# Transposes ahead of the product in the last stage of a six-layer kernel

## The reference

```python
def bitlinear158(x, w, b):
    xq = act_quant(rms_norm(x))      # round(x * 127 / max|x|), 8-bit levels
    wq = weight_quant(w)             # -1, 0, 1 times a scale
    return jnp.einsum('bsd,od->bso', xq, wq) + b
...
h = jax.nn.silu(bitlinear158(x, w1, b1))          # 256 -> 1024
h = jax.nn.gelu(h, approximate=False)
h = layer_norm(h, ln_g, ln_b)
return bitlinear158(h, w2, b2)                    # 1024 -> 256
```

## Time and profile before

| | |
|---|---|
| Time, median of 3 runs | 704.51 us |
| The three runs | 700.71, 704.51, 704.6 us |
| Profiled execution: span from first to last instruction | 711.1 us |
| Profiled execution: a time of its own beside the span | none is given |
| Mean granted TensorE clock of the profiled execution | 0.944 |
| Share of the span: TensorE, VectorE, ScalarE, GpSimd | 87%, 73%, 56%, 47% |
| Second half of the feed-forward, first gelu to the end | 617.4 to 711.1 us |

### The profile page before, as it was taken

One profiled execution on the slowest core, in us unless ns is written; L12 is line 12 of the kernel. 1 busy time (PEld: TensorE's weight loads), 2 busy tenths in 40 slices (PEclk: granted clock), 3 DMA queues, 4 the chain that ended last, 5 costly groups with the idle time before them and its releaser, 6 DMA issues.

```text
span 711.1 us, 15833 instructions
## 1 busy us (share of the span) xinstructions
PE 617.1 (87%) x4620; PEld 471.5 (66%) x4622; DVE 518.5 (73%) x1187; ACT 399.1 (56%) x826; POOL 335.0 (47%) x650
## 2 busy tenths in 40 slices
PE   6999999989998899689999689999999677557776
PEld 5788888875555764477887567888887433245554
DVE  3688999985999674125224569999999578688994
ACT  2577777773333133034332246777777467778992
POOL 1234655444997344411112445333332568475882
PEclk9899999999999799799999779999999899859999
DMA  8301400011348701432221310000000000000101
GB/s 290 129 3 36 168 0 0 0 32 29 67 67 347 260 0 53 141 127 75 78 86 43 142 38 24 2 3 0 0 0 1 1 1 1 0 0 1 35 25 60
DMA packets 23043, 42.07 MB, mean 59 GB/s; under 512 B 3056, under 2 KB 18048, under 8 KB 21840
## 3 DMA queue, kind: packets, MB, share of 16 engines
q1 hardware_dynamic: 19504, 31.14, 13.9%
q0 software_dynamic: 3488, 10.28, 4.3%
HBM read 31.15 MB, written 10.26 MB: 58 GB/s over the span
## 4 chain that ended last, share of the span: by engine, by line
PE 55%; issue 14%; DVE 14%; POOL 8%; ACT 7%; DVEq 1%; DMA 1%; another core or an unknown queue 0%; SPq 0%; POOLq 0%; ACTq 0%
PE ps L1229 6%; PE ps L335 5%; PE ps L363 5%; PE ps L373 4%; PE ps L1109 4%; PE ps L383 3%; PE ps L322 3%; POOL ctx_sb L891 3%; PE ps L345 3%; DVE work L577 3%; PE ps L1239 3%; PE ps L802 2%; PE ps L1162 2%; DVE work L583 2%; PE ps L1883 2%
## 5 line engine op out<-in xcount | busy, mean ns | idle before, releaser
L498 ACT COPY wide<-ps 128x512 f32<-128x512 f32 x126 | 74.5, 593 | 43.3 <-PE ps L335 41.3
L230 POOL TENSOR_TENSOR var_eps<-mv,powers 128x1 f32<-128x1 f32 x80 | 16.8, 210 | 160.6 <-DVE mv L221 160.5
L577 DVE TENSOR_REDUCE work<-ps 128x8 f32<-128x1024 f32 x64 | 77.9, 1217 | 15.4 <-PE ps L322 12.1
L335 PE MATMUL ps<-ident,work 128*128 128x128 f32 x512 | 76.2, 281 | 3.9 <-ACT wide L498 1.8
L493 ACT ACTIVATE work<-work 128x1024 f32<-128x1024 f32 x64 | 68.4, 1069 | 20.0 <-DVE work L583 19.5
L583 DVE TENSOR_TENSOR work<-ps,work 128x1024 f32<-128x1024 f32 x64 | 77.8, 1216 | 0.6
L335 PEld LDWEIGHTS ps<-ident,work 128*128 128x128 f32 x512 | 59.2, 144 | 20.5 <-issue 14.3
L363 PE MATMUL ps<-xnT,w_qkv 128*128 128x128 f32 x256 | 41.0, 309 | 10.8 <-DVE work L583 9.3
L1275 POOL DMA_DIRECT2D sorted_y<-work x23 | 13.6, 591 | 78.0 <-DVE work L1270 78.0
L233 POOL TENSOR_TENSOR rstd<-var_eps,powers 128x1 f32<-128x1 f32 x80 | 45.1, 564 | 6.3
L1883 PE MATMUL ps<-w_o,wide 128*128 128x128 f32 x256 | 34.7, 294 | 15.0 <-DVE w_o L1929 15.0
(11 more groups left out here) (226 smaller groups left out, 1572.9 us busy)
## 6 DMA issues: line engine op xcount, KB each, us to landing
wide<-in_expert_gu SPq DMA_DIRECT2D x1, 4096.0 KB, 15.3
sorted_x<-small POOLq DMA_DIRECT2D x1, 2944.0 KB, 11.7
work<-sorted_x SPq DMA_DIRECT2D x23, 128.0 KB, 2.0
sorted_y<-work POOLq DMA_DIRECT2D x23, 128.0 KB, 2.0
xn_all<-in_ctx_rev_t SPq DMA_DIRECT2D x1, 2048.0 KB, 10.6
small<-hank SPq DMA_DIRECT2D x16, 128.0 KB, 3.8
w_qkv<-hank SPq DMA_DIRECT2D x16, 128.0 KB, 3.8
wide<-in_expert_d SPq DMA_DIRECT2D x1, 2048.0 KB, 9.9
```

The costliest lines, as they stand in the source:

```text
L335: mm = pe.transpose(turned(t, r)[:, h * P:(h + 1) * P], prob[r][:, h * P:(h + 1) * P], ident)
L498: act.copy(probT[r], turned(t, r)).then_inc(s["pT"], 1)
L577: dve.tensor_reduce(mxs[:, 8 * g:8 * g + 8], S2[g], AX.X, ALU.max).then_inc(s["mx"], 1)
```

## The change

In `pe_second` the two blocks of a step change places: `T(t-1)` stands before `Y(t-2)`. ScalarE's `int`, in both halves of the feed-forward, becomes a copy with a constant bias where it was an identity with a bias read from a column. In the first tiles: GpSimd runs `mean(1)` before `rstd(0)`; ScalarE's `var(1)` waits for the mean of tile 1 alone; tile 0's moments have a semaphore of their own, and VectorE goes on to `centred(0)` without counting up `mean` and `var`; the thresholds of the waits on these two follow. In VectorE's step 1 `diag(0)` stands before `ln(1)`. An unused semaphore goes.

```diff
@@ act_first
-                    act.activation(qT[u][:, 0:D], TB[u][:, 0:D], ACT.Identity, bias=c_nmagic
+                    act.activation(qT[u][:, 0:D], TB[u][:, 0:D], ACT.Copy, bias=-MAGIC
...
@@ act_int
-                act.activation(qT[u], TB2[u], ACT.Identity, bias=c_nmagic).then_inc(s["qT"], 1)
+                act.activation(qT[u], TB2[u], ACT.Copy, bias=-MAGIC).then_inc(s["qT"], 1)
@@ act_second
                 if there(t + 1):
-                    act.wait_ge(s["mean"], 2 * (t + 2))
+                    act.wait_ge(s["mean"], 2 * (t + 1))
...
@@ pe_second
-                if there(t - 2):
-                    pe.wait_ge(s["qT"], NB + t - 1)
-                    wait(pe, s["x_new"], t - 3)
-                    for c in range(8):
-                        mm = pe.matmul(Y[u][:, 0:D], qT[u][:, c * P:(c + 1) * P], wq[1][:, c, :],
-                                       start=(c == 0), stop=(c == 7))
-                    mm.then_inc(s["y_ps"], 1)
                 if there(t - 1):
...
                     mm.then_inc(s["qT_ps"], 1)
+                if there(t - 2):
+                    pe.wait_ge(s["qT"], NB + t - 1)
+                    wait(pe, s["x_new"], t - 3)
+                    for c in range(8):
+                        mm = pe.matmul(Y[u][:, 0:D], qT[u][:, c * P:(c + 1) * P], wq[1][:, c, :],
+                                       start=(c == 0), stop=(c == 7))
+                    mm.then_inc(s["y_ps"], 1)
@@ dve_moments
-                dve.bn_aggr(f.mv_buf[:, 0:2], f.bn_buf).then_inc(s["mean"], 2)
-                dve.wait_ge(s["mean"], 2)
-                dve.engine_nop().then_inc(s["var"], 1)
+                dve.bn_aggr(f.mv_buf[:, 0:2], f.bn_buf).then_inc(s["moments"], 1)
+                dve.wait_ge(s["moments"], 1)
@@ dve_second (dve_ln and dve_diag are the old lines, made functions)
+                early = isinstance(t, int) and t == 1
+                if early:
+                    dve_diag(dve, 0, 0)
                 if there(t):
+                    dve_ln(dve, t, u)
+                if there(t - 1) and not early:
+                    dve_diag(dve, t - 1, 1 - u)
@@ gpsimd
-                pool_rstd(pool, 0, 0, f.var[0])
                 pool_mean(pool, 1, 1)
+                pool_rstd(pool, 0, 0, f.var[0])
```

More of the change, by code:

```diff
@@ L175, in build @@
         moe_loaded = sem("moe_loaded")
-        zero_stored = sem("zero_stored")
         out_stored = sem("out_stored")
@@ L1574, in feed_forward @@
                 "factor", "rounded", "diag", "qT_ps", "qT", "h_ps", "silu", "gelu", "mean",
-                "var", "eps2", "rstd", "centred", "ln", "y_ps", "x_bias", "x_new", "h_bias", "unscale")}
+                "var", "eps2", "rstd", "centred", "ln", "y_ps", "x_bias", "x_new", "h_bias", "unscale",
+                "moments")}
             w32 = [xn_all[:, 0:2048], xn_all[:, 2048:4096]]
@@ L1834, in act_gelu @@
             def act_gelu(act, t, u):
-                wait(act, s["mean"], 2 * (t - 1))
+                wait(act, s["mean"], 2 * (t - 2))
                 act.activation(Ht(t), Ht(t), ACT.Gelu, accum_out=hsum[u]).then_inc(s["gelu"], 1)
@@ L1851, in act_second @@
                 if there(t + 2):
-                    wait(act, s["mean"], 2 * (t + 1))
+                    wait(act, s["mean"], 2 * t)
                 if there(t + 1):
@@ L1863, in act_second @@
                     wait(act, s["eps"], NB + t)
-                    wait(act, s["var"], min(t + 2, NB))
+                    wait(act, s["var"], min(t + 1, NB - 1))
                     act.activation(junk, Ht(t), ACT.Square, scale=INNER ** -0.5, accum_out=ms[u]
@@ L1898, in dve_moments, with dve_ln, dve_diag @@
                 dve.wait_ge(f.bn_done, f.base + NB + 2)
-                dve.bn_aggr(f.mv_buf[:, 0:2], f.bn_buf).then_inc(s["mean"], 2)
-                dve.wait_ge(s["mean"], 2)
-                dve.engine_nop().then_inc(s["var"], 1)
+                dve.bn_aggr(f.mv_buf[:, 0:2], f.bn_buf).then_inc(s["moments"], 1)
+                dve.wait_ge(s["moments"], 1)
+            def dve_ln(dve, t, u):
+                dve.wait_ge(s["rstd"], t + 1)
+                dve.wait_ge(s["centred"], t + 1)
+                dve.scalar_tensor_tensor(Ht(t), Ht(t), rstd2[u], ln_b, ALU.mult, ALU.add
+                                         ).then_inc(s["ln"], 1)
+            def dve_diag(dve, t, u):
+                dve_largest(dve, t, u, 1)
+                dve_inverse(dve, t, u, 1)
+                dve.wait_ge(s["inverse"], NB + t + 1)
+                dve.wait_ge(s["rms127"], NB + t + 1)
+                wait(dve, s["qT_ps"], NB + t - 1)
+                dve.tensor_scalar(diag[u], ident, inverse[u], rms127[u], ALU.mult, ALU.mult
+                                  ).then_inc(s["diag"], 1)
             def dve_second(dve, t, u, i):
                 if there(t):
-                    dve.wait_ge(s["var"], t + 1)
+                    wait(dve, s["var"], t)
                     first = isinstance(t, int) and t == 0
@@ L1941, in pool_mean @@
                 pool.tensor_tensor(mean[u], hsum[u], c_inv_n, ALU.mult).then_inc(s["mean"], 1)
-                pool.wait_ge(s["mean"], 2 * t + 1)
-                wait(pool, s["var"], t - 1)
+                pool.wait_ge(s["mean"], 2 * t - 1)
+                wait(pool, s["var"], t - 2)
                 pool.tensor_tensor(nmean32[u], mean[u], c_ninv_rt, ALU.mult).then_inc(s["mean"], 1)
             def pool_rstd(pool, t, u, of=None):
-                pool.wait_ge(s["var"], t + 1)
+                if of is None:
+                    pool.wait_ge(s["var"], t)
+                else:
+                    pool.wait_ge(s["moments"], 1)
                 pool.tensor_tensor(var_e[u], var[u] if of is None else of, c_eps, ALU.add).then_inc(s["eps2"], 1)
@@ L2025, in gpsimd @@
                 pipeline(pool, lambda t, u, i: pool_first(pool, t, u, i), 2, 1, made=IN_MEMORY, first=IN_MEMORY)
+                pool_mean(pool, 1, 1)
                 pool_rstd(pool, 0, 0, f.var[0])
-                pool_mean(pool, 1, 1)
                 pipeline(pool, lambda t, u, i: pool_second(pool, t, u, i), 2, 1)
```

## The result

| | us |
|---|---|
| Kernel before, median of 4 runs on the same chip | 704.56 (700.71 to 704.93) |
| Changed kernel, median of 4 runs | 751.83 (749.97 to 757.51) |
| Ratio, 95% interval | 1.072 (1.068 to 1.077) |
| Changed kernel, profiled execution: time, span | 753.42, 751.7 |
| Mean granted clock of that execution, before 0.944 | 0.896 |

The change makes the kernel 47.3 us slower. Medians are over all runs; ratios compare fast runs alone, since now and then a kernel runs more than 1.5% over its own fastest time. The two profiles differ by 40.6 us in their spans, because the stages ahead of the feed-forward, which the change doesn't touch, took less time in the profile after: the second half starts at 608.6 us, 8.8 us sooner than the 617.4 of before, and the first half's first matmuls (L1770) had already started 11.9 us sooner (548.7 for 560.6).

What follows compares the result with a forecast made beforehand. Before, rings of 4.57 us (TensorE, ScalarE) and 4.62 us (VectorE) bound the stage. x_new(0) at 639.0 + 13 x 7.4 + 7.85 + 3.1 - 0.5 gives 745.6 us profiled, 34.5 more: 739 us median, bounds 719 to 759.

Steps and rivals of the forecast that it cites:

- The ring: Second half, each tile: x_new, ln, diag on VectorE, T, Y on TensorE, x_new again; 7.4 us against 4.57 to 4.62.
- Its length at the high clock: One turn of x_new, ln, diag, T, Y at 2.4 GHz: 5.99 us, with T and Y together 3.37.
- The clock: TensorE's granted clock falls and rises between tiles; half the work at each level, 7.4 us a turn between 6.0 and 8.8.
- always low: Upper bound of a turn, TensorE at 1.2 GHz throughout: 8.8 us, T and Y 6.18; 759 us for the kernel.
- low nearly throughout: Rival: TensorE's clock is low nearly throughout the second half, 750 to 760 us; chance 0.14.
- up and down: The forecast's own case: TensorE's clock goes up and down in the second half, 725 to 752 us; chance 0.60.
- The signs: Profile after: x_new waits 1.4 us or more per tile, VectorE busy 6 or 7 tenths, mean clock near 0.75 for 739.
- The first tiles: Opening of the second half: T(0) 2.2 us sooner, x_new(0) at 639.0 instead of 637.44 us, 1.6 us lost.
- The copy: ScalarE's int: 0.09 us saved on each of 32; first half gains 0 to 1.5 us, 0.5 taken.
- The end: Last tiles, x_new(13) to the last x_new: 6.1 us at the high clock, 9.6 at the low, 7.85 taken.
- The faster rival: Y isn't late if T and Y fit the 2.2 us VectorE leaves between diag and x_new: 699.5 us; chance 0.06.

Runs made afterwards that it cites:

- The order alone: Kernel before with only T(t-1) put before Y(t-2) in TensorE's step: 745.79 us against 692.95 before, ratio 1.075.
- pause filled (7): Changed kernel with 7 filler matmuls into an unused PSUM bank behind each Y on TensorE: 711.78 us against 693.67 before, ratio 1.029.
- change without the order: Changed kernel with Y(t-2) back before T(t-1) on TensorE: 690.04 us against 692.95 for the kernel before, ratio 0.995.
- copy alone: Kernel before with only int made a copy with constant bias, in both halves: 692.31 us against 693.67 before, ratio 0.999.
- x_new a tile later: Changed kernel with x_new(t-4) in place of x_new(t-3) on VectorE, GpSimd's unscale behind its rms: 689.03 us against 693.67 before, ratio 0.991.
- x_new behind diag: Changed kernel with VectorE's x_new(t-3) moved behind diag(t-1): 694.08 us against 692.95 for the kernel before, ratio 0.998.

## Why the prediction was right, and where its sum was off

- **The ring** (part 1) was the right mechanism, on the right engines, at the right place. The order alone gives 1.075 and opening the ring at VectorE's end gives 0.998 with the same list on TensorE.
- **Its length at the high clock**: forecast 5.99 us, measured 6.16 to 6.27 with the pause filled (7). T and Y behind a wait are 3.54 us, not 3.37, and x_new comes 0.14 to 0.25 behind Y, not 0.04.
- **The clock** is the mis-sized term. "I take the middle, 7.4 us: half of this work at each level" was too little. The 13 rings took 110.3 us (630.71 to 740.99), 8.48 each, where 96.2 was forecast: 14.1 us more. With the pause filled (7) they took 80.8. Nearly the whole of T ran at 1.2 GHz in all tiles, and Y in every other one: of the 3.0 us that the low clock adds to T and Y (6.54 against 3.54), 2.26 were paid in the mean ring, three quarters where the forecast had half. That is about 11 of the 14.1 us; the other 3 are the ring's own length. 9.16 us is above even the 8.8 that was named as the end of always low, because T and Y behind a wait take longer than was read from the earlier trace rows: 6.54 us from 675.44 to 681.98, where the forecast had 6.18. The rival "low nearly throughout" (750 to 760 us) had the number, the forecast (up and down, 725 to 752) had the pattern; 751.83 lies on the border of the two. The half had no row behind it but was the middle of two bounds, so what held was the width of the range, not the 739.
- **The signs**: x_new waits 3.18 or 4.45 us where "1.4 us or more" was named, VectorE is busy 5.4 tenths in the mean of the 13 rings where 6 or 7 were, and the clock over the 13 rings is 0.60 in the mean, under the 0.75 that was to go with 739.
- **The first tiles** (part 2): forecast x_new(0) 21.6 us behind the first gelu (639.0 less 617.4) against 20.0; measured 22.1. T(0) was forecast 10.0 us behind it and came at 10.0. That the earlier start is eaten by Y's new place is shown by the change without the order, where x_new(0) comes at 17.7.
- **The copy** (part 3): 0.09 us on each int, as read. The 0.5 us from the first half isn't seen; the measurement of the copy alone can't tell 0 from 1.5 us.
- **The end**: from x_new(13) to the last x_new 7.85 us forecast, 7.63 measured (740.99 to 748.62). The low bound of this term adds up to 9.7 us, not 9.6, which moves nothing.
- Sum: on the stage 35.0 us more were forecast (34.5 with the 0.5 us of the first half) and 49.4 came. Of the 14.4 us between them 14.1 are the rings', about 11 of it the clock, 0.5 the opening, and the end takes 0.2 back.

The rule of the Trainium skill that was weighed ("TensorE: Matmul & The Clock Gate", "HAM oscillation — how this bites in real kernels") agrees with this trace in direction: behind pauses of 2.63 and 2.73 us every T starts at 1.2 GHz. The forecast took the middle between it and the one pause of the trace of before that kept the clock; the measured ring lies near the rule's end.

The faster rival did not come. Its condition, T and Y within the 2.2 us that VectorE leaves, was failed by 1.3 us at the high clock and by over 4 at the low one.

## What to carry to other kernels

Before two blocks change places in an engine's list, follow the block that comes later to the engine that waits for it, and ask what stands behind that wait in the other list: if it feeds the block that was moved ahead, the two lists are now one ring, and the turn of the ring is the sum of both sides. The repair is on the waiting side: take the late result one tile later, in the same slot, so that it still fills the latency between two dependent instructions. And a stall of 1.4 us in each tile on TensorE's partner is not priced at 1.4 us: the pause that it leaves on TensorE can cost it the high clock, which here was one and a half times (by the medians) to twice (by the stages) the price of the stall.

## What was not expected of the hardware

- The clock kept step with the work: in the changed kernel the intervals were 7.9 and 9.16 us in strict turn over five pairs, 17.03 to 17.07 us each (17.07 with the order alone, 7.69 and 9.38).
- Two kernels that differ little fared differently: with a pause of 1.09 us in each 4.62 (x_new a tile later) the clock stayed at 1.00 from 623 us on, with 1.33 in each 4.87 (x_new behind diag) it held from 624 to 651 us and then fell four times. This is one profile of each.
- In the change without the order the clock was low from 601 to 614 us, through T(0), and this cost nothing: T(0) in 3.75 or 2.02 us gives the same x_new(0) to 0.1 us.
